# Self-attention on one core: one ring of seven PSUM banks, the value products between the two score pairs, bias rows later

## The chip, the cores and the metric

The kernel runs on 1 core of a Trainium2 chip. TensorE (PE) multiplies, VectorE (DVE), ScalarE (ACT) and GpSimd (POOL) work on its results, SyncE (SP) and ScalarE start DMAs. The metric is the device time of one execution in microseconds (us); lower is better.

## The reference

The input x is 4 batches of 1024 tokens of width 256. Four layers follow each other: a routed three-expert layer (L0), a transformer block with self-attention, cross-attention and MLP (L1), another such block with adaptive norms (L2), and a cross-attention (L3). The change concerns the two self-attentions, in L1 and L2. For each batch and each of 16 heads of width 16:

```
q, k, v = xm @ Wq + bq, xm @ Wk + bk, xm @ Wv + bv      # 1024 x 256 each
attn    = softmax(q @ k.T / sqrt(16), axis=-1)          # 1024 x 1024 for each head
x       = x + (gate *) (attn @ v @ Wo + bo) + ...       # row of biases added to each token
```

The row of biases of L1 is `silu(cond) @ tp_w + tp_b + bo`, the one of L2 is `gate * bo`, where `gate = silu(cond) @ adaln_w + adaln_b`.

## The kernel before

After a loop over the batches for L0 comes a loop `blocks` of 4 rounds, one for a batch, with 7 modules: L1sa, L1ca, L1mlp, L2sa, L2ca, L2mlp, L3ca. All is in float32; products that take part in the softmax's argument use operands of type fp32r. The order of work is a list of steps, `PASS`, written by `pass_schedule()`. Each engine walks this same list and does its own part of every step, in this order; semaphores that count each engine's finished steps (`mm_done`, `act_done`, `dve_done`, `pool_done`) join them. So the order of steps is the order on every engine.

The steps of a self-attention, for groups g of 4 heads, halves n of 512 queries, t of 4 blocks of 128 queries and kt of 8 blocks of 128 keys:

- `P`, `V`: products for queries, keys and values. `K`: a product with a selection matrix that stacks a pair of heads into the tiles `qs` and `ks` (two heads on rows 0 to 63 and 64 to 127); ACT, or DVE, copies it out.
- `A` (g, n, t, j): scores with queries on the partitions, 128 x 1024 over two banks of PSUM, by two matmuls on the two halves of the array's rows. DVE takes their maximum over the keys (`TENSOR_REDUCE mxh<-ps`, 128 x 1024). There are 16 of them for a (g, n) and 128 for a module. `M` (g, n): DVE joins the halves (`mx<-mxh`), PE turns the tile (`ps<-ident,mx`), ACT copies it to `mrow`, and SP sends four rows by DMA into a row of `qs`, so that the next product subtracts the maximum.
- `S` (g, n, kt, j): scores with keys on the partitions, 128 x 512, one bank, one for a head j; ACT takes the exponential (`probs<-ps`). Heads j = 0 and 1, or 2 and 3, lie on the two halves of the array's rows.
- `PV` (g, n, kt): four products of 32 columns that add up in bank 7, two units after the scores. `O`, `OT`: ACT copies bank 7 out after 8 of them, PE turns it (`ps<-ident,ow`), DVE divides (`rc`, `tok`).
- `R`: the row of biases, products on PE that need `scond` (ACT's SiLU of the condition) and a copy or product on DVE; `add`: POOL adds it to x. `aT`, `o`: the output's transpose and product, `N`: DVE normalises for the next module.

A unit is one (g, n, kt); there are 64 in a module. Its steps stand in the list in this way: A, S of heads 0 and 1, `PV` of two units before, A, S of heads 2 and 3, with an `M` now and then (17 steps of maxima for 8 units). 19 steps of maxima stand ahead between the `K`s and 6 more after them.

Where a step writes in PSUM is fixed when the program is built. Every bank has an owner, the step that reads it last, and `take` makes PE wait for that step. In the self-attentions `single()` gives `S`, `P`, `V`, `K` the banks 4, 5, 6 in turn, and `small()` gives `A` the banks 0 and 1 or 2 and 3 in turn, and the turned tiles bank 0 or 2. In the other modules (`alone`) rings of their own are used, and these don't change.

```
b, act_was, dve_was = take(name, act=name, banks=single())
pe.wait_ge(act_done, upto(act_done, *act_was))
pe.wait_ge(dve_done, upto(dve_done, *dve_was))
```

Of the kernel before, what the change touches and what calls it, by code (L numbers as in the profile page):

```python
# [73 lines left out]
class Marks:  # L74
# [37 lines left out]
    def put(self, step, bank):  # L112
        self.bank[step] = bank
# [10 lines left out]
def pass_schedule():  # L124
# [26 lines left out]
    def self_attention(tag, follow):  # L151
        put(tag, ("P", "k", 0, 1), ("P", "q", 0, 1), ("V", 1), ("K", "dve", "k", 0, 1), ("K", "dve", "k", 1, 1))
        maxima, turn = [], []
        for g in range(GROUPS):
            for n in range(NH):
                scores = [("A", g, n, t, j) for t in range(TPH) for j in range(GH)]

                maxima += scores[:2] + turn + scores[2:]
                turn = [("M", g, n)]
# [5 lines left out]
        def more(upto):  # L165
            nonlocal taken
            upto = min(int(upto), len(maxima))
            put(tag, *maxima[taken:upto])
            taken = max(taken, upto)


        first_slot = GH * TPH + 3
# [3 lines left out]
        rest = beside[first_slot:]  # L176
        for i in range(6):
            put(tag, *rest[2 * i:2 * i + 2])
            more(taken + 1)
        assert len(rest) <= 12  # L180
        put(tag, ("add",))
        ahead, rate, lag = taken, (GH * TPH + 1) / NT, 2
# [3 lines left out]
        for u in range(end + lag):  # L186
            if u < end:
                more(ahead + rate * (u + 0.5))
                put(tag, *[("S",) + units[u] + (j,) for j in range(2)])
            if u < 2:  # L190
                put(tag, ("V", 2 + u))
            if turn is not None:
                put(tag, ("OT",) + turn)
                turn = None
            if u >= lag:
                unit = units[u - lag]
                put(tag, ("PV",) + unit)
                if unit[2] == NT - 1:
                    put(tag, ("O",) + unit[:2])
                    turn = unit[:2]  # L200
            if u < end:
                more(ahead + rate * (u + 1))
                put(tag, *[("S",) + units[u] + (j,) for j in range(2, GH)])

            if u == end - 5:
                put(tag, *[("aT", 0, c) for c in range(KC)])
            elif u in (end - 4, end - 3):
                put(tag, ("o", u - end + 4))
            elif u == end - 1:
                put(follow, ("N", 0))  # L210
# [56 lines left out]
    def mlp(tag, follow):  # L267
# [11 lines left out]
        put(follow, ("R",), *later)  # L279
# [4 lines left out]
    put(tag, ("begin", 0), ("begin", 1), ("N", 0), ("T", 0), ("N", 1), *first, *later, ("T", 1), *rest, ("R",))  # L284
# [48 lines left out]
def build(nc, T, M):  # L333
    ctx = ExitStack()
    with ctx:
# [277 lines left out]
        def _(pe):  # L613
# [220 lines left out]
            rings = {"small": 0, "single": 0, "wide": 0}  # L834
            M.open("blocks")
            with pe.Fori(0, B) as it:
# [4 lines left out]
                for name in PASS:  # L841
# [10 lines left out]

                    def small():
                        rings["small"] += 1
                        if not alone and kind not in ("T", "R", "mod"):
                            b = 2 * (rings["small"] % 2)
                            return b, (b, b + 1) if kind == "A" else (b,)
# [4 lines left out]
                    def single():  # L862
                        rings["single"] += 1
                        if alone:
                            return (2 + rings["single"] % 4,)
                        maxima_done = kind == "S" and PASS.index((tag, "M", GROUPS - 1, NH - 1)) < PASS.index(name)
                        return ((4, 5, 6, 1, 3)[rings["single"] % 5] if maxima_done else 4 + rings["single"] % 3,)
# [4 lines left out]
                    if kind in ("begin", "N", "add", "O", "zero", "context", "out", "split"):  # L872
                        continue
# [458 lines left out]
        def _(dve):  # L1332
# [103 lines left out]
            with dve.Fori(0, B) as it:  # L1436
# [4 lines left out]
                for name in PASS:  # L1441
# [106 lines left out]
                    elif kind == "M" and not cross:  # L1548
# [174 lines left out]
```

## Time and profile before

| what | value |
|---|---|
| median of 3 runs | 4365.98 us (4365.86 to 4377.68) |
| the profiled execution, its own time | 4370.4 us |
| its span (first to last instruction) | 4368.6 us |
| mean granted TensorE clock, share of the full one | 0.951 |
| PE, DVE, ACT busy, share of the span | 89%, 49%, 53% |

Durations below come from the profiled execution. `ps<-ks,qs` names the operands moving first: it is a matmul of an `A` (keys stream against queries held), `ps<-qs,ks` is one of an `S`, `ps<-probs,v` a `PV` (four products are recorded as 8 rows). The shapes of a matmul are rows x columns of the array's part, then what streams. Rows with "x2" merge instructions that follow each other.

### The profile page before, as it was taken

The page shows a single profiled execution, that of the slowest core. Times are in us where ns is not written, and L with a number is a line of the kernel's source. Part 1 is how long each engine was busy: PE and PEld are TensorE (multiplying, and loading weights), DVE is VectorE, ACT ScalarE, POOL GpSimd, SP SyncE. Part 2 cuts the span into 40 slices and gives each one's busy share as a digit, 9 for nine tenths or more (in the row PEclk, how much of TensorE's full clock was granted, in tenths as well). Part 3 has the DMA queues.
Part 4 walks back from the last instruction along what each step waited for, and adds up shares of the span by engine and source line. Part 5 has one row for each costly group of instructions (what it writes and reads, how often), then busy time and mean ns, then how long its engine had stood idle before and what let it go on. Part 6 is the DMA issues. An engine that isn't in the chain of part 4 may idle for free.

```text
span 4368.6 us, 65300 instructions
## 1 busy us (share of the span) xinstructions
PE 3874.2 (89%) x19697; PEld 2181.3 (50%) x19697; DVE 2125.2 (49%) x3461; ACT 2315.6 (53%) x3970; POOL 712.0 (16%) x448
## 2 busy tenths in 40 slices
PE   6999999789888897889988978889889788998888
PEld 4555655334643474336534643356346543563366
DVE  2112111474367454753475437643754467337645
ACT  2122221476467644775476446755765467647754
POOL 1000000100410241004201410024005110140042
PEclk9989989899999998998999989999999899999999
DMA  3000000200000001000000010000000100010000
GB/s 109 18 22 19 10 19 10 67 2 25 30 11 2 11 30 40 2 25 21 20 2 11 30 39 1 16 30 20 1 11 30 39 1 2 26 39 1 1 30 21
DMA packets 90318, 92.58 MB, mean 21 GB/s; under 512 B 28246, under 2 KB 78364, under 8 KB 89884
## 3 DMA queue, kind: packets, MB, share of 16 engines
q1 hardware_dynamic: 61204, 63.43, 4.5%
q10 hardware_dynamic: 28808, 25.17, 1.8%
q8 instruction: 180, 2.95, 0.3%
q14 instruction: 126, 1.03, 0.1%
HBM read 77.80 MB, written 9.44 MB: 20 GB/s over the span
## 4 chain that ended last, share of the span: by engine, by line
issue 64%; PE 18%; POOL 12%; ACT 3%; DVE 2%; DMA 0%; SPq 0%; POOLq 0%; DVEq 0%; ACTq 0%
PE ps L618 17%; POOL hidl L1645 3%; ACT probs L1300 3%; POOL x L1636 2%; DVE mxh L1546 1%; POOL ql L1663 1%; POOL small L1584 1%; POOL hTl L1591 1%; POOL kl L1663 1%; POOL W2h L1654 1%; POOL W1h L1654 1%; PE ps L1038 1%; PE ps L993 0%; POOL W1l L1656 0%; POOL W2l L1656 0%
## 5 line engine op out<-in xcount | busy, mean ns | idle before, releaser
L1300 ACT ACTIVATE probs<-ps 128x512 f32<-128x512 f32 (+1 forms) x2176 | 1192.3, 636 | 438.9 <-PE ps L618 436.2
L1546 DVE TENSOR_REDUCE mxh<-ps 128x2 f32<-128x1024 f32 x1024 | 1202.6, 1220 | 342.6 <-PE ps L618 337.6
L618 PE MATMUL ps<-probs,v 128*32 128x512 f32 (+1 forms) x4864 | 652.8, 609 | 3.8 <-ACT probs L1300 3.8
L618 PE MATMUL ps<-qs,ks 64*128 64x512 f32 x2048 | 589.8, 430 | 68.3 <-ACT probs L1300 68.3
L1584 POOL TENSOR_TENSOR small<-small 128x4 f32<-128x4 f32 x64 | 66.9, 1046 | 2961.4 <-DVE small L1345 2961.4
L618 PE MATMUL ps<-ks,qs 64*128 64x512 f32 x2048 | 466.2, 459 | 54.1 <-DVE mxh L1546 45.8
L618 PEld LDWEIGHTS ps<-ks,qs 64*128 64x128 f32 x2048 | 187.8, 183 | 507.3 <-issue 281.0
L618 PEld LDWEIGHTS ps<-qs,ks 64*128 64x128 f32 x2048 | 268.6, 184 | 329.2 <-ACT probs L1300 287.5
L618 PE MATMUL ps<-hT,slot 128*128 128x512 f32 x448 | 228.9, 653 | 33.3 <-ACT hT L1105 33.3
L1273 ACT ACTIVATE qs<-ps,cols 128x512 fp32r<-128x512 f32 x320 | 214.0, 688 | 70.2 <-PE ps L618 69.6
L1543 DVE TENSOR_REDUCE mx<-ps 128x4 f32<-128x312 f32 x384 | 164.4, 477 | 145.3 <-PE ps L618 143.1
L618 PE MATMUL ps<-slot,hT 128*128 128x256 f32 x896 | 217.1, 389 | 14.8 <-ACT hT L1311 9.3
L618 PEld LDWEIGHTS ps<-slot,hT 128*128 128x128 f32 x896 | 164.6, 191 | 66.0 <-issue 16.5
L1424 DVE SCALAR_TENSOR_TENSOR sg<-sg,ps 128x512 f32<-128x512 f32 x16 | 11.0, 688 | 350.7 <-PE ps L618 350.7
L1158 ACT ACTIVATE hid<-ps,cols 128x512 f32<-128x512 f32 x112 | 77.0, 689 | 190.6 <-PE ps L618 190.4
L1663 POOL TENSOR_TENSOR ql<-whole,qh 128x512 fp32r<-128x512 f32 x80 | 102.1, 1276 | 452.2 <-ACT whole L1262 452.2
L618 PEld LDWEIGHTS ps<-probs,v 128*32 128x32 f32 (+1 forms) x4864 | 96.1, 108 | 153.3 <-issue 107.8
L618 PE MATMUL ps<-hid,ew 128*128 128x512 f32 x384 | 169.1, 596 | 0.0
L618 PE MATMUL ps<-qh,sel 128*128 128x512 f32 x320 | 153.3, 479 | 12.7 <-POOL ql L1663 7.0
L1645 POOL TENSOR_TENSOR hidl<-hid,hidh 128x512 fp32r<-128x512 f32 x128 | 161.0, 1288 | 9.6 <-ACT hid L1318 8.9
L618 PE MATMUL ps<-qs,kz 128*77 128x512 f32 x384 | 135.9, 457 | 28.9 <-DMA qs<-mrow 18.0
L1571 DVE RECIPROCAL rc<-ps 128x16 f32<-128x16 f32 x160 | 40.6, 254 | 246.9 <-PE ps L1038 246.9
(210 smaller groups left out, 6038.3 us busy)
## 6 DMA issues: line engine op xcount, KB each, us to landing
qs<-mrow SPq DMA_DIRECT2D x640, 2.0 KB, 1.7
slot<-in_L_w SPq DMA_DIRECT2D x8, 1024.0 KB, 7.2
slot<-in_L_fc_w SPq DMA_DIRECT2D x8, 1024.0 KB, 5.1
adw<-in_L_adaln_w SPq DMA_DIRECT2D x4, 1536.0 KB, 6.6
xin<-in_x ACTq DMA_DIRECT2D x5, 1024.0 KB, 5.5
x_after_block<-x ACTq DMA_DIRECT2D x20, 256.0 KB, 2.2
xin<-x_after_block ACTq DMA_DIRECT2D x5, 1024.0 KB, 5.5
ew<-in_L_e_w SPq DMA_DIRECT2D x6, 768.0 KB, 13.5
```

The source lines that it names most:

```text
L618: return pe.matmul(out, lhsT, rhs, start=start, stop=stop)
L1038: ins = pe.transpose(ps[:, a, i * P:(i + 1) * P], ow[:, o:o + P], ident[:])
L1158: act.activation(hid0[:, m, :], ps[:, M.where(("L0", "h", n, m)), :], ACT.Silu, bias=col("L0_e_b1", m)).then_inc(act_done, M.add(act_done, ...
L1273: act.activation(qs[:, pair, n * HALF:(n + 1) * HALF], ps[:, M.where(name), :], ACT.Identity, bias=qs_rows).then_inc(act_done, M.add(act_d ...
L1300: ins = act.activation(dst, src, ACT.Exp, scale=SCALE)
L1543: dve.tensor_reduce(mx[:, z, t, j0:j0 + GH], ps[:, a, 0:GH * SP_].rearrange("p (j s) -> p j s", s=SP_), AX.X, ALU.max, negate=True).then_i ...
L1546: dve.tensor_reduce(mxh[:, z, t, j // 2, j % 2, :], ps[:, a:a + 2, :], AX.X, ALU.max, negate=True).then_inc(dve_done, M.add(dve_done, name))
L1584: pool.tensor_tensor(rstd[:, tt], ve[:, tt], nhalf[:, tt], ALU.pow).then_inc(pool_done, M.add(pool_done, (tag, "rstd", h)))
L1636: pool.tensor_tensor(x[:], xin[:] if tag == "L1sa" else x[:], rrow[:].unsqueeze(1).to_broadcast([P, NT, D]), ALU.add).then_inc(pool_done, ...
L1645: pool.tensor_tensor(hidl[:, n, m, :], hid[:, n, m, :], hidh[:, n, m, :].bitcast(F32), ALU.subtract).then_inc(pool_done, M.add(pool_done, ...
L1654: pool.tensor_tensor(hi[:], w, zero.unsqueeze(2).to_broadcast(w.shape), ALU.add).then_inc(pool_done, M.add(pool_done, name + ("hi",)))
L1663: pool.tensor_tensor(lo[:, c, part], whole[:, whole_of(name)[0], 0:kn], hi[:, c, part].bitcast(F32), ALU.subtract).then_inc(pool_done, M.a ...
```

## The change

Four things. In a unit, both `A`s now stand together at its end, so that the list reads S 0, S 1, `PV`, S 2, S 3, A, A; two `A`s for a unit, whatever the `M`s; and 20 + 6 `A`s stand ahead of the first unit in place of 25 steps of maxima. The step `M` is split: `both` (DVE's part) stands after two `A`s of the next (g, n), `M` (the turn) after two more. `R` of the two self-attentions moves from the module's head to a place just ahead of its first unit. And in the self-attentions all steps but `PV` take banks from one pool of seven: `shared` gives the bank, or pair of neighbours, whose last use is oldest. The output's steps at the end of the units stand one unit later.

```
-                maxima += scores[:2] + turn + scores[2:]
-                turn = [("M", g, n)]
+                maxima += scores[:2] + turn[:1] + scores[2:4] + turn[1:] + scores[4:]
+                turn = [("both", g, n), ("M", g, n)]
...
         def more(upto):
+
             nonlocal taken
-            upto = min(int(upto), len(maxima))
-            put(tag, *maxima[taken:upto])
-            taken = max(taken, upto)
-
-
-        first_slot = GH * TPH + 3
+            while taken < len(maxima) and (maxima[taken][0] != "A" or sum(m[0] == "A" for m in maxima[:taken]) < upto):
+                put(tag, maxima[taken])
+                taken += 1
+
+        first_slot = GH * TPH + 4
...
+        lead = first_slot + 6
         for i in range(6):
             put(tag, *rest[2 * i:2 * i + 2])
-            more(taken + 1)
+            more(first_slot + i + 1)
         assert len(rest) <= 12
-        put(tag, ("add",))
-        ahead, rate, lag = taken, (GH * TPH + 1) / NT, 2
+        put(tag, ("R",), ("add",))
+        lag = 2
...
             if u < end:
-                more(ahead + rate * (u + 0.5))
                 put(tag, *[("S",) + units[u] + (j,) for j in range(2)])
...
             if u < end:
-                more(ahead + rate * (u + 1))
                 put(tag, *[("S",) + units[u] + (j,) for j in range(2, GH)])
-
-            if u == end - 5:
+                more(lead + 2 * (u + 1))
+
+            if u == end - 4:
                 put(tag, *[("aT", 0, c) for c in range(KC)])
-            elif u in (end - 4, end - 3):
-                put(tag, ("o", u - end + 4))
-            elif u == end - 1:
+            elif u in (end - 3, end - 2):
+                put(tag, ("o", u - end + 3))
+            elif u == end:
                 put(follow, ("N", 0))
...
-        put(follow, ("R",), *later)
+        put(follow, *[("R",)] * (KIND[follow] == "cross"), *later)
...
+                    def shared(count):
+
+                        b = min(range(8 - count), key=lambda i: max(used[i:i + count]))
+                        used[b:b + count] = [max(used) + (1 if count == 1 else 3)] * count
+                        return tuple(range(b, b + count))
+
                     def small():
+                        if not alone:
+                            banks = shared(2 if kind == "A" else 1)
+                            return banks[0], banks
                         rings["small"] += 1
-                        if not alone and kind not in ("T", "R", "mod"):
-                            b = 2 * (rings["small"] % 2)
-                            return b, (b, b + 1) if kind == "A" else (b,)
...
                     def single():
+                        if not alone:
+                            return shared(1)
                         rings["single"] += 1
-                        if alone:
-                            return (2 + rings["single"] % 4,)
-                        maxima_done = kind == "S" and PASS.index((tag, "M", GROUPS - 1, NH - 1)) < PASS.index(name)
-                        return ((4, 5, 6, 1, 3)[rings["single"] % 5] if maxima_done else 4 + rings["single"] % 3,)
+                        return (2 + rings["single"] % 4,)
```

On PE, one unit in the middle of L1sa, as it stands before, from an `A` to the `PV` of the next unit (the lines without operands set the number that a wait compares with):

```order
L618 MATMUL ps<-ks,qs 128x512 x2
L1005 REGISTER_ALU
L618 MATMUL ps<-qs,ks 128x512
L1005 REGISTER_ALU
L618 MATMUL ps<-qs,ks 128x512
L973 REGISTER_ALU
L618 MATMUL ps<-ks,qs 128x512 x2
L1005 REGISTER_ALU
L618 MATMUL ps<-qs,ks 128x512
L1005 REGISTER_ALU
L618 MATMUL ps<-qs,ks 128x512
L618 MATMUL ps<-probs,v 32x512 x4
```

And the same place in the changed program:

```order
L618 MATMUL ps<-qs,ks 128x512
L1012 REGISTER_ALU
L618 MATMUL ps<-qs,ks 128x512
L979 REGISTER_ALU
L618 MATMUL ps<-ks,qs 128x512 x2
L978 REGISTER_ALU
L618 MATMUL ps<-ks,qs 128x512 x2
L618 MATMUL ps<-qs,ks 128x512
L1011 REGISTER_ALU
L618 MATMUL ps<-qs,ks 128x512
L618 MATMUL ps<-probs,v 32x512 x4
```

The number of matmuls of a unit is the same; the second `A` has moved across the pair of `S`, so the two `A`s stand next to each other, and the pairs of `S` stand on either side of `PV`.

On PE, the head of L1sa before, after the first values (`ps<-slot_91,hT`); `ps<-slot_94,scond` and `ps<-rows,ident` are `R`:

```order
L618 MATMUL ps<-slot_91,hT 128x256 x4
L889 ISA
L893 REGISTER_ALU
L618 MATMUL ps<-slot_94,scond 128x256 x2
L618 MATMUL ps<-rows,ident 128x256 x2
L935 REGISTER_ALU
L618 MATMUL ps<-hT,slot_91 128x512 x2
```

In the changed program `R` stands here, between the last `A` ahead of the units and the first `S`:

```order
L979 REGISTER_ALU
L618 MATMUL ps<-ks,qs 128x512 x4
L978 REGISTER_ALU
L618 MATMUL ps<-ks,qs 128x512 x2
L895 ISA
L899 REGISTER_ALU
L618 MATMUL ps<-slot_94,scond 128x256 x2
L618 MATMUL ps<-rows,ident 128x256 x2
L1003 ISA
L1012 REGISTER_ALU
L618 MATMUL ps<-qs,ks 128x512 x2
```

The four products of `R` are the same; they have moved behind the `K`s and the first 26 `A`s.

## Rows read from the trace of the kernel before

**Rows 1.** The page: span, and busy time by engine.

```profile
span 4368.6 us, 65300 instructions
PE 3874.2 (89%) x19697; PEld 2181.3 (50%) x19697; DVE 2125.2 (49%) x3461; ACT 2315.6 (53%) x3970; POOL 712.0 (16%) x448
```

**Rows 2.** A window of 100 us, busy us (instructions) of PE, PEld, DVE, ACT, POOL; PEclk.

```profile
900.00:1000.00 100.00, 86.75 (x545) 34.65 (x544) 77.66 (x76) 70.73 (x136) 0.00 (x0) 1.00 0.01 2
```

**Rows 3.** Timeline, one unit: start, us, engine, operation, idle before it and releaser.

```profile
906.65 1.06 PE L618 MATMUL ps<-probs,v 128*32 128x512 f32 x8
907.65 0.50 PE L618 MATMUL ps<-ks,qs 64*128 64x512 f32 x2
907.98 0.39 PE L618 MATMUL ps<-qs,ks 64*128 64x512 f32 x2
908.22 0.40 PE L618 MATMUL ps<-ks,qs 64*128 64x512 f32 x2
908.41 2.06 ACT L1300 ACTIVATE probs<-ps 128x512 f32<-128x512 f32 x4 [0.77 <-PE ps L618]
908.45 0.39 PE L618 MATMUL ps<-qs,ks 64*128 64x512 f32 x1
909.06 0.49 PE L618 MATMUL ps<-qs,ks 64*128 64x512 f32 x1 [0.22 <-ACT probs L1300]
909.48 1.07 PE L618 MATMUL ps<-probs,v 128*32 128x512 f32 x8
```

**Rows 4.** Timeline, the next unit, where an `A` waits for a maximum.

```profile
910.48 0.73 PE L618 MATMUL ps<-ks,qs 64*128 64x512 f32 x4
911.02 2.36 DVE L1546 TENSOR_REDUCE mxh<-ps 128x2 f32<-128x1024 f32 x2 [0.48 <-PE ps L618]
912.30 0.50 PE L618 MATMUL ps<-ks,qs 64*128 64x512 f32 x2 [0.81 <-DVE mxh L1546]
912.64 0.56 PE L618 MATMUL ps<-qs,ks 64*128 64x512 f32 x2
```

**Rows 5.** The line of the maxima in the window 900 to 1000: busy us, mean ns.

```profile
L1546 DVE TENSOR_REDUCE mxh<-ps 128x2 f32<-128x1024 f32 x64 | 75.5, 1220 | 22.2 <-PE ps L618 21.8
```

**Rows 6.** Timeline, a turn of maxima (`M`) and its DMAs.

```profile
902.64 0.17 DVE L1555 TENSOR_TENSOR mx<-mxh 128x16 f32<-128x16 f32 x1
902.86 0.60 PE L993 MATMUL ps<-ident,mx 128*4 128x128 f32 x4 [1.17 <-DVE mx L1555]
903.38 0.50 PE L618 MATMUL ps<-qs,ks 64*128 64x512 f32 x2
904.19 3.34 SPq L575 DMA_DIRECT2D qs<-mrow  x4
```

**Rows 7.** Timeline: the first `PV` of two turns of 8 units, and a turned output.

```profile
894.30 1.06 PE L618 MATMUL ps<-probs,v 128*32 128x512 f32 x8
...
918.80 0.66 PE L1038 MATMUL ps<-ident,ow 128*128 128x128 f32 x4
919.39 1.06 PE L618 MATMUL ps<-probs,v 128*32 128x512 f32 x8
```

**Rows 8.** The page, DMA issues: KB each, median us to landing.

```profile
qs<-mrow SPq DMA_DIRECT2D x640, 2.0 KB, 1.7
```

**Rows 9.** Timeline, `R` in the head of L1sa, first round.

```profile
813.60 1.28 ACT L1242 ACT_TABLE_LOAD   x1
814.89 0.20 ACT L1242 ACTIVATE scond<-cond 128x2 f32<-128x2 f32 x1
815.15 1.13 PE L618 MATMUL ps<-slot,scond 128*128 128x256 f32 x4 [2.20 <-ACT scond L1242]
817.92 0.50 PEld L618 LDWEIGHTS ps<-hT,slot 128*128 128x128 f32 x2 [0.65 <-issue]
```

**Rows 10.** Timeline, the last `A` ahead of the units of L1sa.

```profile
860.69 0.50 PE L618 MATMUL ps<-ks,qs 64*128 64x512 f32 x2 [0.63 <-DVE mxh L1546]
```

**Rows 11.** Timeline, PE at the first output product after L2sa's units.

```profile
1464.62 1.56 PE L618 MATMUL ps<-slot,hT 128*128 128x256 f32 x6 [1.36 <-ACT whole L1262]
```

More of the change, by code:

```diff
@@ L283, in pass_schedule @@
     first, later, rest = head(KIND[tag])
-    put(tag, ("begin", 0), ("begin", 1), ("N", 0), ("T", 0), ("N", 1), *first, *later, ("T", 1), *rest, ("R",))
+    put(tag, ("begin", 0), ("begin", 1), ("N", 0), ("T", 0), ("N", 1), *first, *later, ("T", 1), *rest)
     for i, (tag, kind) in enumerate(MODULES):
@@ L834, in _ @@
             rings = {"small": 0, "single": 0, "wide": 0}
+            used = [0] * 7
             M.open("blocks")
@@ L871, in _ @@
                         pe.wait_ge(SLOT_OF[tag], upto(SLOT_OF[tag], LAST_LOAD[tag]))
-                    if kind in ("begin", "N", "add", "O", "zero", "context", "out", "split"):
+                    if kind in ("begin", "N", "add", "O", "both", "zero", "context", "out", "split"):
                         continue
@@ L1547, in _ @@
                                               ).then_inc(dve_done, M.add(dve_done, name))
-                    elif kind == "M" and not cross:
+                    elif kind == "both":
                         g, n = step[1:]
```

## The prediction

> **What bounds the kernel now.** I read the page first: PE is busy 89% of the span, DVE 49%, ACT 53% [rows 1]. That looks like a kernel bound by TensorE, but the share is a mean over modules, and a matmul's end in the trace is modelled. So the second view was the window in the middle of a self-attention [rows 2]: PE 86.8 us of 100, DVE 77.7, ACT 70.7, granted clock 1.00. No engine is full, so something hands over late. The third view was the timeline of one unit [rows 3], where starts say more than durations. `PV` takes 1.00 us from its start to the next (906.65 to 907.65); the first pair of matmuls behind it 0.33 (907.65 to 907.98); a pair that follows a pair 0.24 (907.98 to 908.22), because the two matmuls of a pair lie on different halves of the array and run together; a pair to the next `PV` takes 0.42 (909.06 to 909.48). Then the loss: `S` of head 0 starts at 908.45, but head 1 starts alone at 909.06, released by ACT. It wants one of the banks 4, 5, 6, and its bank is still owned by the `S` of head 2, whose exponential began at 908.41. Without this wait the two would be one pair at 908.45, and `PV` would follow at 908.87 and not 909.48: 0.61 us lost in a unit of 2.83.
>
> So a unit needs of PE 1.00 + 0.33 + 0.24 + 0.24 + 0.42 = 2.23 us; of DVE two maxima at 2.36 - 1.22 = 1.14 us from start to start [rows 4, 5], 2.28; of ACT four exponentials at (2.06 - 0.60)/3 = 0.49 [rows 3], 1.95, where 0.60 is the length of one (2.06 for four). A turn of 8 units, the period of the pattern, takes 919.39 - 894.30 = 25.09 us [rows 7], or 3.14 a unit: five units of 2.83, one with `M`, one with `OT`, and one in which a third `A` comes (17 steps of maxima for 8 units) and PE waits 0.81 for DVE [rows 4]. The waits that end last are thus the S bank (ACT) and, in three units of 8, DVE's handover.
>
> **The change, part by part.** *The units.* Now the pairs of `S` keep their partner, since seven banks are shared and a bank comes back after about one unit and not after three scores. The 0.61 goes. What is late next is the pair of `A`s. They need 4 banks at once out of 7 and take the oldest; writing out the bank list by hand, the first `A` of a unit nearly always gets a bank that the second `A` of the unit before had. That gives a loop: `A` starts, DVE starts 0.54 later (910.48 to 911.02 [rows 4]), its second maximum starts 1.14 after, lasts 1.22 [rows 5], and PE starts 0.05 after its end (911.02 + 1.22 to 912.30 gives 0.06 [rows 4]): 0.54 + 1.14 + 1.22 + 0.05 = 2.95 us from first `A` to first `A`. On PE alone the same way is 1.00 + 0.33 + 0.34 (an `A` that has waited, 912.30 to 912.64 [rows 4]) + 0.24 + 0.42 = 2.34, so such a unit waits 0.61 at its first `A`: as much as before at `S`, but for two maxima in the unit. Where DVE is ahead (it gains about 0.7 in each unit with an `M` or an `OT`, where PE has more to do), the wait is shorter: with about 0.25 left the unit is 2.6, without any 2.2 to 2.3.
>
> I walked the list of steps with these durations and the banks, engine by engine. The same walk of the list before gives 2.83, 3.88, 3.57, 3.52 for the plain, `M`, third-`A` and `OT` units and 25.1 for the turn, against 25.09 in the trace, so I trust it to some tenths of a turn. For the changed list it gives a turn of an `M` unit of 3.66 (2.95 and the turned tile, 0.52 from 902.86 to 903.38 [rows 6], and the switch back), an `OT` unit of 3.63 (0.59 [rows 7] on top), and six plain units that add up to 16.2 (three at 2.95, two or three at 2.6, one near 2.3): 23.5. Gain 25.1 - 23.5 = 1.6 for 8 units. Six turns of a module have maxima in them: 9.6 us. Against this, maxima end two or three units later (two a unit and not 2.1), and there PE waits once for the last `M`: 0.9. Net 8.7 us a module. The 14 units behind them have no `A` and go by ACT in both kernels: nothing.
>
> *`M` two to four `A`s later.* SP issues the DMAs that bring the maxima into `qs`. From `M` to the first `S` of the next group the list before gives 912.64 - 902.86 = 9.8 us [rows 4, 6], my walk of the new one 8.6. The chain needs 904.19 - 902.86 + 3.34 (four issues) + 1.7 (landing) = 6.4 [rows 6, 8]. Hidden, with 2.2 to spare.
>
> *`R` of L1sa.* In the head PE stands still for 2.20 until ACT has loaded a table (1.28) and made `scond` (0.20), and then works until 817.92 [rows 9]: the block costs 817.92 - 815.15 + 2.20 = 4.97. Its first two products take 1.13 with their tail, so I put all four at 1.9 where the clock is full. All of 4.97 goes from the head (5.3 with what ACT then has ready earlier). It returns ahead of the first `S`: ACT must finish the last `K`, load, and make `scond`, while PE runs out of `A`s; PE waits about 1.1 and works 1.9, but of the waits of 0.2 and 0.6 for DVE at the last `A`s of before [rows 10] and of one step less ahead of the units 1.4 is given back. Net +1.6. Together -3.7. DVE's copies (some 0.7) fall into PE's wait.
>
> The Trainium skill, "ScalarE: Activation LUTs", section "What ACT_TABLE_LOAD costs", puts a switch of tables at 1.28 us and a drain of 1.38 behind it. Here `scond` starts 0.01 after the load's end [rows 9], so the trace shows no such drain; by the page the wait of PE ahead of the units would be 1.4 longer in each of 4 rounds and the sum 5.5 smaller. I go by the row.
>
> *`R` of L2sa.* `scond` exists, so nothing waits: 1.9 leaves the head, and 1.9 less DVE waits returns, -1.3 net.
>
> *The tail.* Behind the units of L2sa the first output product wants a bank whose owner is ACT's copy for the next module's queries: PE waits 1.36 [rows 11]. The pool gives it another bank; with what follows in step -2.1. L1sa has no such wait: -0.1.
>
> Sum for a round: L1sa -3.7 - 8.7 - 0.1 = -12.5; L2sa -1.3 - 9.1 (its end of maxima loses less) - 2.1 = -12.5; together -25, in 4 rounds -100 us. The profiled execution took 4370.4 us (span 4368.6 and 1.8 around it), so 4270; the median of the runs is 4.4 below that execution, which gives **4266 us**, 2.3% less.
>
> **The rivals.** *The units give nothing* (the change doesn't do what it says). If every plain unit falls into the loop of 2.95, the turn is 6 x 2.95 + 3.66 + 3.63 = 25.0 as before, and with the 0.9 the units gain nothing. Left are the heads and tails, 3.7 + 0.1 + 1.3 + 2.1 = 7.2 a round, less the 0.9 of either module: between 22 and 29 us, so about 4340. For it: nearly every first `A` does meet a bank of the unit before. Against it: the `M` and `OT` units let DVE catch up 0.7 each, which must shorten the units behind them. Chance 0.15.
>
> *DVE stays ahead.* If the extra of an `M` or `OT` unit carries further and six plain units take 2.6 each, the turn is 22.9, 0.6 x 6 x 8 = 29 more than forecast: 4237; the floor of PE (2.23) is not reached, as DVE alone needs 2.28. Chance 0.08.
>
> *Slower: the clock.* PE now stops at the `A` for 0.6 in half of the units, at a new place, and rotates through seven banks. If that let the granted clock fall to the lower level, 1.2 GHz, PE's part of a plain unit would be 1.00 + 0.33 + 0.34 + 0.24 + 0.42 with its streaming doubled, about 4.2 us. Each such unit costs 1.3 more than forecast; the 1.6 of a turn is gone when more than 1.2 of 8 units run so, and if half of them did, 50 x 8 x 0.5 x 1.3 = 260 us come on top, 4526. Against it: with stops of 0.6 in nearly every unit the granted clock was 1.00 in the window [rows 2]. Chance 0.03. The Trainium skill, "TensorE: Matmul & The Clock Gate", section "A second HAM failure mode: psum-queue depth-cycling", tells of a kernel that cycles through banks and whose small idle times make the clock swing; by it the changed kernel would be this rival, and by it the kernel before should show it too, which the row does not.
>
> *Slower: maxima land late.* If the DMAs take over 2.2 us more than in the trace, each turn pays the excess; it decides from 3.8 on. The median landing is steady at 1.7 [rows 8]. Chance 0.02.
>
> **How the numbers follow.** Forecast 0.72, the others as above. The likeliest's own range: 0.4 us a turn either way (48 turns x 0.4 = 19 us) and 2 us a round for the heads and tails (8 us) give 4240 to 4293. For 8 in 10 it reaches down to the case with DVE ahead (4237, with its own spread 4232) and up somewhat over halfway to the case without gain in the units: 4232 to 4310. 0.3%, or 13 us, is about what can be told from no change. Slower than that takes the last two rivals or their like: 0.04. Within it: units without gain and the `R` costing ahead of the units what it saved in the head: 0.05. Faster: 0.91.
>
> **What would show it.** In the trace after: the single `ps<-qs,ks` released by ACT is gone, all are x2; `ps<-ks,qs` x4 (merged pairs) wait 0.2 to 0.6 for `mxh`; a turn from `OT` to `OT` takes 23.5; in the window DVE is busy near 84 and PE near 92 (the same work in 23.5 and not 25.1); in the head of L1sa no `ACT_TABLE_LOAD` with PE idle, but one ahead of the first `S`, PE idle about 1.1; in L2sa's tail no wait for `whole`; the modules between unchanged. Wrong would be: plain units all at 2.95 or more, `S` waiting for ACT again, a granted clock under 1 in the window, or `S` waiting for the DMAs.

## The result, and the profile after

The changed kernel takes 4257.36 us (4247.97 to 4265.01) against 4365.92 for the kernel before, a ratio of 0.9745 [0.9701, 0.9788]. One more execution of 9187.91 us was left out of all comparisons. The profiled execution took 4247.97 us, so the difference of the two profiled executions, 4370.4 - 4247.97 = 122.4, is larger than that of the medians, 108.6. The page of the changed kernel, span and busy time, which answer to [rows 1]:

```profile
span 4246.2 us, 65032 instructions
PE 3811.6 (90%) x19697; PEld 2171.6 (51%) x19697; DVE 2120.0 (50%) x3461; ACT 2326.9 (55%) x3970; POOL 712.1 (17%) x448
```

*Where the time went.* I marked in both traces the first `hT,slot` product behind L0, and in every self-attention the first `A`, the first `S` and the last `S`. Means over the four rounds, in us:

| stretch | before | after | difference | forecast |
|---|---|---|---|---|
| L0, up to the mark | 797.13 | 775.55 | -21.6 | 0 |
| head of the first L1sa (mark to first `A`) | 30.88 | 21.44 | -9.4 | -5.3 |
| L1sa, first `A` to first `S` | 33.02 | 35.07 | +2.05 | +1.6 |
| L2sa, the same | 33.05 | 33.49 | +0.44 | +0.6 |
| L1sa, first to last `S` | 192.95 | 187.09 | -5.9 | -8.7 |
| L2sa, the same | 192.89 | 186.52 | -6.4 | -9.1 |
| last `S` of L1sa to first `A` of L2sa | 176.46 | 171.73 | -4.7 | -2.0 |
| last `S` of L2sa to first `A` of the next L1sa | 268.09 | 256.92 | -11.2 | -7.4 |

The first two rows count once, the next five four times, the last three times. Without L0 that is -9.4 + 4 x (2.05 + 0.44 - 5.9 - 6.4 - 4.7) - 3 x 11.2 = -101, where the forecast was -100. Behind the last of these marks the two traces take the same time; 2.1 of the forecast should have come there. L0's code is the same in both kernels; its length was 772 to 779 us in six of this study's profiled kernels and 797 to 798 in three (before, and two of the experiments), with more or less time at half clock: 122.9 to 127.6 us of it in the three long ones (127.4 before), 58.7 to 63.6 in the six short ones (59.3 after). Two of the three long ones are kernels with the changed order or the pool, so those 21.6 us are most likely chance of one execution and not the change; with one profile for each kernel this is argued and not shown.

*The units.* The timeline of PE in the changed kernel, a unit and its neighbour, which answer to [rows 3, 4], and ahead of them the turned output that starts this turn of 8 units, the turned maxima in it, and the next turned output behind them:

```profile
888.61 0.66 PE L1044 MATMUL ps<-ident,ow 128*128 128x128 f32 x4
...
896.44 0.74 PE L618 MATMUL ps<-ks,qs 64*128 64x512 f32 x4 [0.52 <-DVE mxh L1552]
897.12 0.60 PE L999 MATMUL ps<-ident,mx 128*4 128x128 f32 x4
...
903.29 1.07 PE L618 MATMUL ps<-probs,v 128*32 128x512 f32 x8
904.29 0.49 PE L618 MATMUL ps<-qs,ks 64*128 64x512 f32 x2
905.31 0.73 PE L618 MATMUL ps<-ks,qs 64*128 64x512 f32 x4 [0.53 <-DVE mxh L1552]
905.89 0.53 PE L618 MATMUL ps<-qs,ks 64*128 64x512 f32 x2
906.35 1.06 PE L618 MATMUL ps<-probs,v 128*32 128x512 f32 x8
...
912.15 0.66 PE L1044 MATMUL ps<-ident,ow 128*128 128x128 f32 x4
```

Every `ps<-qs,ks` is now a pair (x2). The idle time stands in front of the merged `A`s and is DVE's; from 905.31 to the `A` of the next unit (908.27) it is 2.96, the loop forecast at 2.95. The turn from `OT` to `OT` is 912.15 - 888.61 = 23.54; the five turns with maxima in this module are 23.92, 23.54, 23.64, 23.92 and 23.52, mean 23.71, before 25.1. The windows (columns as in [rows 2]) of this turn, and of the same 100 us as in [rows 2]:

```profile
888.60:912.15 23.55, 21.30 (x137) 9.09 (x136) 19.41 (x20) 18.08 (x34) 0.00 (x0) 1.00 0.01 2
900.00:1000.00 100.00, 90.25 (x568) 36.10 (x565) 73.30 (x72) 75.73 (x145) 0.00 (x0) 0.98 0.05 17
```

In the turn DVE is busy 19.41 of 23.55 us, 82%, and PE 21.30, 90% (forecast 84 and 92). DVE falls in the window of 100 us, since the last maxima lie in it (at 988) and nothing follows them. The waits of PE over all units of this L1sa, first before, then after (line waited for, us in total, times, longest):

```profile
PE ps L618 <- ACT probs L1300: 8.5, 39, 0.2
PE ps L993 <- DVE mx L1555: 8.3, 7, 1.3
PE ps L618 <- DVE mxh L1546: 5.5, 7, 0.8
```

```profile
PE ps L618 <- DVE mxh L1552: 10.8, 29, 0.5
PE ps L999 <- DVE mx L1561: 2.0, 1, 2.0
PE ps L618 <- ACT probs L1306: 2.0, 5, 0.5
PE ps L1044 <- ACT ow L1312: 1.5, 1, 1.5
```

Seven waits for a joined maximum (8.3) have become one (2.0), ACT's 8.5 has become 2.0, and DVE's maxima wait 10.8 and not 5.5. That one wait is the end of the maxima, and something follows it that was not forecast:

```profile
988.41 0.60 PE L999 MATMUL ps<-ident,mx 128*4 128x128 f32 x4 [2.04 <-DVE mx L1561]
988.93 0.50 PE L618 MATMUL ps<-qs,ks 64*128 64x512 f32 x2
989.37 1.94 PE L618 MATMUL ps<-probs,v 128*32 128x512 f32 x8
```

A `PV` of 1.94 where others take 1.06 is one at half clock: 3.4 us at the lower of the two levels (1.2 and not 2.4 GHz). Such a stretch stands behind the last maxima in all eight self-attentions of the changed kernel, where the last `M` waits 2.04 in L1sa and 2.43 in L2sa, and in none of before, where it waits 1.30.

*The row of biases.* The timeline ahead of the units of L1sa, where [rows 9, 10] stood before:

```profile
828.39 1.28 ACT L1248 ACT_TABLE_LOAD   x1
829.69 0.20 ACT L1248 ACTIVATE scond<-cond 128x2 f32<-128x2 f32 x1
829.94 1.13 PE L618 MATMUL ps<-slot,scond 128*128 128x256 f32 x4 [1.24 <-ACT scond L1248]
...
832.06 0.60 PE L618 MATMUL ps<-qs,ks 64*128 64x512 f32 x2
832.60 3.52 PE L618 MATMUL ps<-slot,hT 128*128 128x256 f32 x8
```

PE waits 1.24 (forecast 1.1), works from 829.94 to 832.06 = 2.12 (forecast 1.9). The first `V` among the units takes 3.52 where the next takes 1.99: half clock again, in this round and the third, not in the other two. The first `OT` comes 32.6 us behind the first `S` here, and 31.0 where the clock stays up, so the stretch costs 1.6.

In the head that `R` has left, one more thing changed that was not in the forecast. Before, the granted clock falls behind the wait of 2.20 for `scond`; this is a window of the kernel before (columns as in [rows 2]):

```profile
816.50:823.30 6.80, 6.80 (x11) 2.93 (x11) 0.58 (x3) 1.27 (x2) 0.22 (x1) 0.50 0.00 0
```

These 6.8 us at half clock stand in the head of L1sa in all four rounds before. In the changed kernel, and in the other five with `R` moved, there is no half clock in the 14 us ahead of L1sa's first `A`.

*The tail of L2sa.* PE at the first output product ([rows 11] before), at the next product that waits, and at the first product for the queries of L2ca, first after, then before:

```profile
1416.66 3.62 PE L618 MATMUL ps<-slot,hT 128*128 128x256 f32 x16
1422.18 0.69 PE L618 MATMUL ps<-rows,ident 15*128 15x256 f32 x2 [1.90 <-DVE x L1523]
1422.80 3.67 PE L618 MATMUL ps<-hT,slot 128*128 128x512 f32 x4
...
1427.12 0.47 PE L618 MATMUL ps<-qh,sel 128*128 128x512 f32 x1
```

```profile
1471.52 0.48 PE L618 MATMUL ps<-qh,sel 128*128 128x512 f32 x1
```

The 1.36 for `whole` is gone, and a wait of 1.90 for DVE's sum stands behind it. Behind that wait the clock is at half again (0.50 from 1422.8 to 1426.2): the four `hT,slot` products take 3.67 and not 1.99. From the last `S` to the first output product it took 10.64 us and now takes 7.66; but to the first `qh,sel` it took 17.54 and now takes 18.11, the same in all four rounds. So the tail as a whole gained nothing: it lost 0.6.

### The profile page after: what moved, and what is told of

Same layout as the page of the kernel before. It is cut to its first block, busy times and chain, and to the rows that moved or that the text cites. A ratio compares the mean times of both kernels' runs of the same rounds, so it can differ in the third digit from the quotient of the medians.

```text
span 4246.2 us, 65032 instructions
## 1 busy us (share of the span) xinstructions
PE 3811.6 (90%) x19697; PEld 2171.6 (51%) x19697; DVE 2120.0 (50%) x3461; ACT 2326.9 (55%) x3970; POOL 712.1 (17%) x448
## 4 chain that ended last, share of the span: by engine, by line
issue 85%; POOL 13%; PE 1%; DMA 0%; POOLq 0%; SPq 0%; DVE 0%; ACT 0%; DVEq 0%; ACTq 0%
POOL hidl L1651 3%; POOL x L1642 2%; POOL ql L1669 2%; POOL small L1590 2%; POOL hTl L1597 1%; POOL kl L1669 1%; PE ps L618 1%; POOL W2h L1660 1%; POOL W1h L1660 1%; POOL W2l L1662 0%; POOL W1l L1662 0%; DMA gw<-in_L_gate_w 0%; POOL ew1h L1607 0%; PE ps L1044 0%; SPq L575 0%
## 5 line engine op out<-in xcount | busy, mean ns | idle before, releaser
L1306 ACT ACTIVATE probs<-ps 128x512 f32<-128x512 f32 (+1 forms) x2176 | 1214.1, 635 | 381.9 <-PE ps L618 377.9
L618 PE MATMUL ps<-qs,ks 64*128 64x512 f32 x2048 | 529.8, 472 | 0.0
L618 PE MATMUL ps<-ks,qs 64*128 64x512 f32 x2048 | 412.7, 454 | 113.3 <-DVE mxh L1552 87.0
L618 PEld LDWEIGHTS ps<-qs,ks 64*128 64x128 f32 x2048 | 254.9, 185 | 490.6 <-ACT probs L1306 349.4
L618 PE MATMUL ps<-qs,kz 128*77 128x512 f32 x384 | 130.0, 442 | 30.9 <-DMA qs<-mrow 23.2
```

Of the source, the lines that this page charges most:

```text
L618: return pe.matmul(out, lhsT, rhs, start=start, stop=stop)
L1306: ins = act.activation(dst, src, ACT.Exp, scale=SCALE)
```

## The experiments

All ratios are to the kernel before, run on the same chip; the medians of before lie between 4352.47 and 4362.37, so that kernels of different chips are better compared by ratio than by median. The first four take the change apart.

**`R` moved, nothing else** (old order, old banks).

```
-        put(tag, ("add",))
+        put(tag, ("R",), ("add",))
...
-        put(follow, ("R",), *later)
+        put(follow, *[("R",)] * (KIND[follow] == "cross"), *later)
```

> The kernel before with R alone moved ahead of the units. Theory (the heads gain, because PE has no idle time there and its clock stays up): the block of 4.97 us leaves L1sa's head and about 4 us of half-clock time with it, 3 to 4 us come back ahead of the units; L2sa even. 4 to 7 us a round, 16 to 28 us faster than before, about 4345. Rival (the clock in the head was chance between two runs): 4 us faster at most, 4362.

Measured: 4337.74, ratio 0.9954 [0.9928, 0.9979], so 20 us less (9 to 31); by the marks, without L0, 11 less. The turn stays 25.1. The first head is 22.65 and not 30.88, and ahead of the first `S` 4.4 us come back in L1sa and 2.9 in L2sa, then 1.6 and 1.1 in the units: more than the 1.6 and 0.6 forecast, since in this kernel the granted clock falls at `R` in all four rounds (in the first behind its wait of 1.21 for `scond`), and stays low into the first units (`R` takes 832.03 to 835.60, 3.57 and not 2.12). The theory of the expectation holds for the head: the 6.8 us at half clock that stood in L1sa's head before are gone in every round. What follows: alone the move gives 11 to 20 where 20 was forecast, and both halves are larger, in L1sa -8 and +6 in place of -5.3 and +1.6. The stretch from L1sa to L2sa loses 3.9 and the one from L2sa to the next L1sa 9.3, where the forecast had 1.9 and 5.3 for the leaving of `R`.

**The changed kernel with `R` back in the heads.**

```
-        put(tag, ("R",), ("add",))
+        put(tag, ("add",))
...
-        put(follow, *[("R",)] * (KIND[follow] == "cross"), *later)
+        put(follow, ("R",), *later)
```

> The changed kernel with R back in the heads; units, maxima and banks as changed. Theory: loses what e1 gains, 16 to 28 us against the changed kernel (4257), so 4273 to 4285, and the half-clock stretch of 3.4 us at the first unit of L1sa is gone. Rival: the same as the changed kernel within 5 us.

Measured: 4270.93, ratio 0.9798 [0.9760, 0.9836]; above the changed kernel, whose ratio is 0.9745, by 13.6 us in the medians and 23 in the ratios (the intervals overlap). The stretch at half clock at the first unit is gone, as expected. By the marks, from this kernel to the changed one the stretches between the modules lose 3.6 and 6.0, those ahead of the first `S` gain 3.8 and 2.3, and the units lose 0.4 and 1.4: -5.3 a round. This is not quite the forecast's -5.0. The 1.8 in the units lies in stretches at half clock behind the last `M`, where the forecast put nothing; without them it is -3.5. And the -5.0 held 1.4 and 1.3 of DVE's waits given back, which this kernel has given back already: it takes 31.3 and 31.2 from first `A` to first `S`, where the kernel before takes 33.0 in both. So the move by itself was forecast at about -2.3 a round and measured at about -3.5. The sign holds; the head gives more than forecast. Here 0 to 6.8 us at half clock stand in L1sa's head behind the wait for `scond` (2.5), and none with `R` moved.

**The new order on the old banks** (`single()` and `small()` as before).

```
-                    def shared(count):
...
-                        if not alone:
-                            return shared(1)
                         rings["single"] += 1
-                        return (2 + rings["single"] % 4,)
+                        if alone:
+                            return (2 + rings["single"] % 4,)
```

> The changed kernel with the old banks: scores in 4, 5, 6, maxima in 0 and 1 or 2 and 3. My prediction held that the pool of seven is what takes away the wait of the second score: then the scores wait again and the units stay near 3.1 us, about 4330. Rival: the order alone does it, since PV now stands between the two pairs and gives ACT the time to free a bank; and the second pair of banks of the maxima is then always free in time: units of 2.6, a turn of 8 units near 23.3 us against 23.7 of the changed kernel, 4260 to 4280.

Measured: 4284.04, ratio 0.9825 [0.9779, 0.9871]. The timeline of PE: a turned output, a unit in the middle, and the next turned output.

```profile
913.88 0.66 PE L1039 MATMUL ps<-ident,ow 128*128 128x128 f32 x4 [0.28 <-DVE mxh L1547]
...
931.50 1.07 PE L618 MATMUL ps<-probs,v 128*32 128x512 f32 x8
932.49 0.50 PE L618 MATMUL ps<-qs,ks 64*128 64x512 f32 x2
932.83 0.74 PE L618 MATMUL ps<-ks,qs 64*128 64x512 f32 x4
933.41 0.77 PE L618 MATMUL ps<-qs,ks 64*128 64x512 f32 x2
934.11 1.06 PE L618 MATMUL ps<-probs,v 128*32 128x512 f32 x8
...
937.16 0.66 PE L1039 MATMUL ps<-ident,ow 128*128 128x128 f32 x4 [0.28 <-DVE mxh L1547]
```

The turn is 23.28, shorter than the changed kernel's 23.71, and the plain unit 934.11 - 931.50 = 2.61. No `A` shows a wait here: the two `A`s of a unit take banks 0, 1 and 2, 3 in turn, so each wants the banks of the `A` two before it. The maximum of the first is over in good time; that of the second ends at 933.02, and the second `A` of the next unit starts at 933.07, just in time.

The wait at the `S` is smaller, but it is not gone. The pair at 933.41 lasts 0.77, because its second matmul starts only at 933.68, 0.05 after the exponential that began at 933.02 is over (0.60 later): 0.27 where it was 0.61. The profile's list of waits leaves it out, being so short. Added up over the 64 units of the first L1sa, the second matmul of the pair starts 25.5 us behind the first in the kernel before, 15.4 us in this one and 5.2 in the changed one. So the order takes away 10 us of it and the pool another 10. But the pool puts waits of the `A`s in its place (10.8 us, here none), while here the turned tiles wait for the banks of a maximum (0.98 at an `M`, 0.28 at an `OT`). From first to last `S` the modules take 184.3 and 185.1, that is 8.7 and 7.8 less than before. What the pool adds shows by the marks against the changed kernel: -2.0 and -2.2 between the modules, -1.4 and -3.4 ahead of the first `S`, +2.8 and +1.5 in the units; -4.7 a round, 19 us in all, where the medians differ by 26.7. The intervals overlap, so that the pool helps at all rests on the marks; and those are from one execution each, of which this one has 287.7 us at half clock outside L0 and the units and the changed kernel's 253.9, worth up to 17 of the 19. That the pool helps in the changed kernel is thus not shown; that it costs in the units is (turns of 23.71 against 23.28). The order is itself several moves (`A`s in pairs, two to a unit, 26 ahead, `M` later), of which only the last was taken out alone.

**The pool of seven on the old order.**

```
+                    def shared(count):
+
+                        b = min(range(8 - count), key=lambda i: max(used[i:i + count]))
+                        used[b:b + count] = [max(used) + (1 if count == 1 else 3)] * count
+                        return tuple(range(b, b + count))
```

> The kernel before with the pool of seven banks alone, order as before. If the pool takes the score's wait away, a unit of 2.83 loses 0.4 to 0.6 us and the whole is 50 to 150 us faster. Rival: without the order the oldest banks are those that DVE still reads; scores wait for DVE 0.6 to 0.8 us in each unit, a turn takes 28 us and the kernel is about 190 us slower, 4550.

Measured: 4559.54, ratio 1.0435 [1.0391, 1.0480]: slower than the kernel before. The timeline of PE in a unit, a second place 17 us on, and the window of one turn (its seventh column is the granted clock):

```profile
928.92 0.39 PE L618 MATMUL ps<-qs,ks 64*128 64x512 f32 x2
929.15 0.39 PE L618 MATMUL ps<-ks,qs 64*128 64x512 f32 x2
929.38 0.39 PE L618 MATMUL ps<-qs,ks 64*128 64x512 f32 x1
930.40 0.49 PE L618 MATMUL ps<-qs,ks 64*128 64x512 f32 x1 [0.63 <-DVE mxh L1552]
...
947.63 0.51 PE L618 MATMUL ps<-ks,qs 64*128 64x512 f32 x2 [0.71 <-DVE mxh L1552]
948.76 0.49 PE L618 MATMUL ps<-qs,ks 64*128 64x512 f32 x1 [0.40 <-DVE mxh L1552]
...
953.29 1.93 PE L618 MATMUL ps<-probs,v 128*32 128x512 f32 x8
```

```profile
927.60:958.30 30.70, 25.12 (x140) 9.87 (x139) 19.71 (x20) 18.37 (x35) 0.00 (x0) 0.89 0.01 2
```

The `S` of head 1 is torn from its pair as before, but now it waits for DVE's maximum (0.63), not for ACT's exponential: the oldest bank is one that an `A` had, and DVE is slower to give it back. This turn is 30.7. In it the granted clock falls, mean 0.89: 0.11 / 0.5 x 30.7 = 6.8 us at half clock, behind waits of 0.2 to 1.2. Turns of this kernel in which the clock stays up take 28.7, so the waits cost 3.6 of a turn and the clock up to 2 more. So the pool without the new order loses: seven banks do not by themselves end the wait at the `S`, which is what the prediction had them do.

**The maxima's turn not moved** (`both` and `M` directly behind the first two `A`s, the rest as changed).

```
-                maxima += scores[:2] + turn[:1] + scores[2:4] + turn[1:] + scores[4:]
+                maxima += scores[:2] + turn + scores[2:]
```

> The changed kernel with both halves of M after the second A of the next group, as before the change. Theory: with two A's side by side DVE is two maxima behind when PE reaches the turned tile, so PE waits about 2.3 us there in each turn of 8 units and loses its lead: a turn near 26.3, 33 us a round, about 4390. Rival: DVE has caught up by then, the turn stays at 23.7 and the kernel at 4257.

Measured: 4449.9, ratio 1.0220 [1.0177, 1.0264], 193 us slower than the changed kernel by the medians and more than either the theory (4390) or its rival (4257) had. PE at the turned maxima and behind them, the output that ends the turn, and windows ahead of and behind the start of `M`:

```profile
901.34 0.66 PE L1044 MATMUL ps<-ident,ow 128*128 128x128 f32 x4
...
909.25 0.69 PE L999 MATMUL ps<-ident,mx 128*4 128x128 f32 x4 [2.04 <-DVE mx L1561]
...
910.60 1.93 PE L618 MATMUL ps<-probs,v 128*32 128x512 f32 x8
...
928.75 0.66 PE L1044 MATMUL ps<-ident,ow 128*128 128x128 f32 x4
```

```profile
900.00:909.25 9.25, 6.74 (x40) 2.98 (x40) 7.97 (x10) 5.26 (x11) 0.00 (x0) 1.00 0.01 3
909.25:912.65 3.40, 3.40 (x16) 0.93 (x18) 0.00 (x0) 1.67 (x3) 0.00 (x0) 0.56 0.01 1
```

This turn is 27.41 (all with maxima lie between 27.2 and 27.5), 3.7 more than in the changed kernel. 2.04 of it is the wait of PE for two maxima and their joining; the rest goes with the half clock behind it (0.56 over 3.4 us), in which DVE stands idle for 4.30 until the next `A`. The last `M` of the changed kernel waits the same 2.04 and is followed by the same stretch: this run shows it behind 46 of its 48 `M`s ahead of the last ones (waits of 1.94 to 2.31), which ties the stretch to the wait. It is no certainty, though: the last `M`s here wait 2.43, and only three of eight are followed by one. With the `A`s in pairs, leaving `M` where it was costs more than the whole change gives: in the pool of seven, the split and later `M` is what makes the new order pay. With the old banks this was not tried.

**Banks split by kind** (`A`s in 0, 1 or 2, 3, everything else the oldest of 4 to 6 while `A`s are left, then of all seven; otherwise as changed).

```
-                        b = min(range(8 - count), key=lambda i: max(used[i:i + count]))
-                        used[b:b + count] = [max(used) + (1 if count == 1 else 3)] * count
+                        if count == 2:
+                            b = 0 if max(used[0:2]) <= max(used[2:4]) else 2
+                        else:
+                            b = min(range(4, 7) if any(k[:2] == (tag, "A") for k in PASS[PASS.index(name):]) else range(7), key=lambda i: used[i])
+                        used[b:b + count] = [max(used) + 1] * count
```

> The changed kernel with the pool divided while maxima are left in the module: A takes 0 and 1 or 2 and 3, all others the oldest of 4, 5, 6; afterwards all seven. Theory (the loop of 2.95 comes from a first A that meets a bank of the second A of the unit before, and the pool pays outside of the units): plain units of 2.6, a turn of 22.0, 13 us a round less than the changed kernel, about 4205. Rival: scores wait for ACT in three banks as long as A waited for DVE; a turn of 23.3 as in e3, about 4245.

Measured: 4194.43, ratio 0.9641 [0.9605, 0.9677]; its interval lies below that of the changed kernel. PE from one turned output to the next, and its waits over all units of L1sa (as above):

```profile
883.46 0.66 PE L1047 MATMUL ps<-ident,ow 128*128 128x128 f32 x4
...
905.50 0.66 PE L1047 MATMUL ps<-ident,ow 128*128 128x128 f32 x4
```

```profile
PE ps L1002 <- DVE mx L1564: 2.4, 1, 2.4
PE ps L1047 <- ACT ow L1315: 1.5, 1, 1.5
```

The turn is 22.04. Nothing waits for a maximum but the last `M`: 3.9 us of listed waits in a module in place of 16.3 in the changed kernel (10.8 + 2.0 + 2.0 and 1.5 for the last output). Not listed, being short, are those of the `S` pairs: their second matmul starts 15.0 us behind the first, added up over the module, as in the order on the old banks, and not 5.2. Against that order (23.28) the turn is 1.24 shorter. It is where the turned tiles go: there `M` and `OT` take bank 0 or 2 behind a maximum and wait 0.98 + 0.28, here they don't.

**The same with `scond` at the start of the round.**

```
+                        act.wait_ge(conditions_loaded, upto(conditions_loaded, "all"))
+                        act.activation(scond[:], cond[:], ACT.Silu).then_inc(act_done, M.add(act_done, "scond"))
...
-                    elif kind == "R" and tag == "L1sa":
-                        act.wait_ge(conditions_loaded, upto(conditions_loaded, "all"))
-                        act.activation(scond[:], cond[:], ACT.Silu).then_inc(act_done, M.add(act_done, "scond"))
```

> As e6, and ACT makes scond at the start of the round, where it waits for the first transposes anyway. Theory: PE's wait of 1.24 us at R ahead of the units and the half-clock stretch behind it (V at 3.5 us in place of 2.0) go: 2 to 3 us a round, 8 to 12 us less than e6. Rival: PE only reaches DVE's maxima earlier and waits there: within 4 us of e6.

Measured: 4189.66, ratio 0.9660 [0.9620, 0.9699], the same as without it. From first `A` to first `S` of L1sa it takes 34.7 where it took 34.8. In both kernels the last `A` ahead of `R` waits 1.07 for DVE, and with the pool split the load is over by then; PE waits for DVE there and not for the table.

## Why the prediction was right, and where it was not

The forecast was 4266 for a measured 4257.36, inside the range, and -100 us for the profiled execution without L0 against -101. But errors cancel in that sum, and that it came out within 1 us is luck: the units gave 22 us less than forecast and the tails some 11 less, and the heads and the modules between gave about as much more.

*The units: right in kind, a third too large.* Forecast -8.7 and -9.1 a module, measured -5.9 and -6.4: 22 us less in all. In the first L1sa the five turns between outputs gave 5 x 25.1 - 118.5 = 7.0 where 8.0 was forecast (23.7 a turn and not 23.5). The end of the maxima cost 1.9 (the turn behind them takes 21.27, before 19.38) where I had put 0.9: the 3.4 us at half clock behind the last `M` were not in the walk. They are 1.2 to 1.6 of it: with the order on the old banks, where the last `M` waits 2.43 in all eight modules, that turn takes 19.9 in the four without a stretch and 21.1 to 21.5 in the four with one. And the first turn, which gave its 1.6 elsewhere, gave nothing in the two L1sa whose `V` runs at half clock. 8.7 less 1.0, less 1.0, less 1.6 there is 5.1, as measured in that module (192.9 to 187.9); where `V` keeps its clock, 6.6.

*The cause of the gain in the units: half wrong.* "Now the pairs of `S` keep their partner, since seven banks are shared and a bank comes back after about one unit" is the step that failed. The 0.61 was put to the banks, and the order was given no part in it. The order alone on the old banks takes away 10 of the 25.5 us that the second `S` of the pairs comes late in a module and gives the better turn (23.28); the pool alone makes the wait longer (turns of 28.7 to 30.9). In the new order the pool does take away another 10, so that most pairs keep their partner as forecast, but it pays for them at the `A`s, through the loop that I did describe, and the turn is 0.4 longer for it. That loop itself held: `A`s merged, waiting 0.2 to 0.5, 2.96 from one to the next where two units in a row fall into it.

*`M` later: hidden as forecast, but not free to leave out.* No `S` waits for SP or for a DMA in the changed kernel. I costed it as if only its chain mattered, and not what PE would wait at it in the new order: 3.7 a turn.

*`R`: right in sign, and its head too small.* The wait behind the table's load was 1.24 (forecast 1.1) and the work 2.12 (1.9). What was put at nothing is the clock behind the old wait: the 4.97 of the block was all that was to leave the head, but 6.8 us at half clock behind the 2.20 left with it in every round, worth up to 3.4. The first head lost 9.4 where 5.3 was forecast, 8.2 of it with `R` moved alone. By the Trainium skill, "ScalarE: Activation LUTs", section "What ACT_TABLE_LOAD costs", a switch of tables costs a drain of 1.38 us on top of the load. The rows again show only the load: `scond` starts 0.02 us behind its end (828.39 + 1.28 to 829.69), so the measurement decides against the drain here.

*The tail of L2sa: wrong.* The wait for `whole` is gone and the first output product comes 3.0 earlier, as forecast. But the -2.1 took it that what follows moves with it. PE waits 1.90 for DVE's `x` instead, 3.4 us at half clock follow, and the first product of L2ca's queries comes 0.6 later than before. The last tail of the program agrees: the two traces take the same time there, where 2.1 was forecast. Why `x` comes late is not shown; in the pool on the old order, and in the kernel with `R` back, nothing waits for it and the same product comes 2.0 and 1.6 earlier than before. So the forecast 2.1 was there to be had, and with one pool it hung on where `R` stands.

*The stretches between the modules: too small.* "The modules between unchanged" was the second sentence that failed. The heads and the stretches behind the units gave -9.4 - 4 x 4.7 - 3 x 11.2 = -61.8, forecast -5.3 - 4 x 2.0 - 3 x 7.4 = -35.5. With the tails giving nothing, even more than the difference of 26 is to be explained. Part of it is `R` leaving the heads: in the two pairs of kernels that differ by `R` alone the stretch from L1sa to L2sa loses 3.9 and 3.6 (forecast 1.9), and the one from L2sa to the next L1sa 9.3 and 6.0 (forecast 5.3). All time at half clock outside L0 and the units fell from 300.1 to 253.9 us (the granted clock summed over the trace), and 27 of these 46 are the 6.8 in the four heads of L1sa; at one half speed 46 us are worth up to 23. The mean granted clock of the first head rose from 0.80 to 0.87, and moving `R` alone brings it to 0.89. Which of the other stretches gained because of the change and which by chance I can't tell: stretches of 3.4 us come and go there between kernels whose code is the same at that place.

*The rivals.* "Units give nothing": not so, the turn is 23.7 and not 25.0. "DVE stays ahead" (22.9 a turn) is not what the changed kernel does; it is what the split banks reach (22.04). "Maxima land late": nothing of it. "Slower by the clock" was half right: in the turns the clock is 1.00, but at the end of the maxima, and at `R`, it does fall. The Trainium skill, "TensorE: Matmul & The Clock Gate", section "A second HAM failure mode: psum-queue depth-cycling", which I had set aside, describes short idle times that let the clock swing; the changed kernel's turns do not show it, with waits of 0.2 to 0.5 in more than half of the units, and the pool on the old order does, with 0.89 in the turn shown, though even there waits cost more than the clock.

## What to carry to other kernels

In the units, one pool of PSUM banks with the oldest taken was not better than rings by kind (turns of 23.7 and 23.3): it couples a fast consumer to the slowest. Give the slow consumer (here two maxima of 1.22 us) banks of its own, in turns, and let everything else share the others; here the ratio to the kernel before went from 0.9745 to 0.9641, 45 us. When a change is made of an order and a pool, try each alone before saying which one pays: they had opposite signs. Cost a long wait on PE with the clock that may fall behind it, not only with its own length. And follow a wait that is taken away to the next product that waits for something else: in L2sa's tail all of it came back.

## What the runs showed of the hardware

The granted clock often falls to half for 3.4 or 6.8 us behind a single longer wait of PE. Of the waits at the `M`s inside the units, in all nine kernels, 96 lasted 1.79 to 2.44 us, and with 77 of them such a stretch began, some 0.6 us ahead of the wait's end at the earliest; 216 lasted 0.97 to 1.30, and with none of them one did. At the same length it can go either way: 2.43 at the last `M` was followed by one in four of eight modules with the order on the old banks, in seven of eight with the banks split. At other places shorter waits were enough at times: the 1.24 to 1.26 at `R` in two of four rounds of the changed kernel, the 1.2 at `R` moved alone in four of four. The 2.20 in the head before and the 1.90 in the tail after were followed by one in four of four. In the pool on the old order the clock fell in the units with no wait above 1.3 there. A `PV` takes 1.93 to 1.94 at half clock and not 1.06, the `V` of eight products 3.52 and not 1.99. The order of work can thus move the time by more than its waits: in the kernel with `M` early, 552.1 us of the execution ran at half clock, in the changed one 350.7, in the one before 427.5.
